# A gated linear-attention layer with a complex feed-forward layer: squares on ScalarE, grouped edge copies, a causal mask made in two places, and sums of squares in column tiles

## The reference

```
mixed = x @ W_qkv.T                      # 3072 channels: q, k, v, 16 heads of 64 each
mixed = silu(causal depthwise conv, 4 taps, of mixed)
q, k = l2norm(q) * 64**-0.5, l2norm(k)   # per head
beta = sigmoid(x @ W_b.T); g = -exp(A_log) * softplus(x @ W_a.T + dt_bias)
S_t = S_{t-1} * exp(g_t) + k_t (v_t * beta_t)^T ;  o_t = q_t S_t
out = o * rsqrt(mean(o*o) + 1e-6) * silu(x @ W_z.T);  y = out @ W_out.T
ffn: W_real, W_imag (512 x 512) unfolded from small factors;
     out_real = xr @ Wr.T - xi @ Wi.T + bias_real, out_imag = xr @ Wi.T + xi @ Wr.T + bias_imag
```

## Time and profile before

| | us |
|---|---|
| median of 3 runs (lowest, highest) | 971.15 (971.06, 973.98) |
| the profiled execution, its own time | 975.45 |
| its span, slowest core (7) | 973.7 |
| PE, DVE, POOL, ACT busy on core 7 | 737.8, 461.4, 274.6, 264.9 |
| mean granted TensorE clock, core 7 | 0.900 |

### The profile page before, as it was taken

One profiled execution on the slowest core, in us unless ns is written; L12 is line 12 of the kernel. 1 busy time (PEld: TensorE's weight loads), 2 busy tenths in 40 slices (PEclk: granted clock), 3 DMA queues, 4 the chain that ended last, 5 costly groups with the idle time before them and its releaser, 6 DMA issues.

```text
span 973.7 us, 15242 instructions; the slowest of 8 cores (947.4 to 973.7 us)
## 1 busy us (share of the span) xinstructions
PE 737.8 (76%) x4912; PEld 337.0 (35%) x4912; DVE 461.4 (47%) x716; ACT 264.9 (27%) x445; POOL 274.6 (28%) x551
## 2 busy tenths in 40 slices
PE   0345768787877977978784888899879999787755
PEld 0111323343433432424331334344333444344311
DVE  0623345574845665525420534654436455455522
ACT  0121232342333423322331232233223334221100
POOL 2023213315133233142312342313244133222210
PEclk9967869999999979999997979899979999977777
DMA  5876555565465773635767525437526345422311
GB/s 122 166 158 140 114 140 168 131 163 163 130 163 131 182 189 110 196 117 136 149 171 190 180 61 152 123 107 191 148 77 163 87 122 150 113 77 78 76 54 54
DMA packets 113285, 129.98 MB, mean 133 GB/s; under 512 B 56228, under 2 KB 76588, under 8 KB 113072
## 3 DMA queue, kind: packets, MB, share of 16 engines
q1 hardware_dynamic: 103056, 107.78, 39.9%
q0 software_dynamic: 10144, 21.15, 11.8%
HBM read 110.02 MB, written 18.27 MB: 132 GB/s over the span
## 4 chain that ended last, share of the span: by engine, by line
PE 54%; DVE 11%; DMA 11%; issue 8%; ACT 6%; POOL 6%; SPq 2%; DVEq 0%; POOLq 0%; ACTq 0%
PE pR L448 23%; PE pR L506 10%; PE pB L862 5%; POOL s_ksq L519 4%; PE pA L896 4%; DMA wscr<-s_w 4%; ACT s_post L512 2%; DVE s_ktil L685 2%; DMA s_lnxT<-s_lnx 2%; DMA dscr<-s_d 2%; SPq L131 2%; ACT L512 1%; DVE s_pre L480 1%; ACT L397 1%; PE pB L760 1%
## 5 line engine op out<-in xcount | busy, mean ns | idle before, releaser
L448 PE MATMUL pR<-s_lnxT,s_w 128*128 128x512 bf16 x1408 | 341.0, 396 | 26.7 <-DMA s_w<-wcat 13.8
L448 PEld LDWEIGHTS pR<-s_lnxT,s_w 128*128 128x128 bf16 x1408 | 136.9, 101 | 195.6 <-issue 58.0
L506 PE MATMUL pR<-s_pre,s_d 128*128 128x512 bf16 x608 | 166.2, 409 | 24.0 <-DVE s_pre L480 14.2
L480 DVE CAST s_pre<-pR 128x512 bf16<-128x512 f32 x152 | 104.3, 687 | 64.8 <-PE pR L448 64.7
L512 ACT ACTIVATE s_post<-pR 128x512 bf16<-128x512 f32 x152 | 86.2, 596 | 133.8 <-PE pR L506 133.4
L483 POOL COPY s_halo<-s_pre 128x3 bf16<-128x3 bf16 x152 | 47.0, 309 | 260.9 <-DVE s_pre L480 254.2
L512 ACT ACT_TABLE_LOAD x32 | 41.1, 1283 | 197.7 <-PE pR L506 197.7
L506 PEld LDWEIGHTS pR<-s_pre,s_d 128*128 128x128 bf16 x608 | 54.7, 102 | 100.5 <-issue 50.8
L519 POOL TENSOR_TENSOR s_ksq<-s_post 128x512 bf16<-128x512 bf16 x64 | 67.4, 1061 | 53.7 <-ACT s_post L512 51.6
L816 DVE TENSOR_TENSOR s_S<-s_S,pA 128x512 f32<-128x512 f32 x32 | 21.9, 685 | 124.5 <-POOL s_S L793 103.4
L492 PE MATMUL pG<-s_ksq,s_bones 128*32 128x128 bf16 x256 | 16.7, 248 | 81.3 <-POOL s_ksq L519 81.3
(11 more groups left out here) (124 smaller groups left out, 814.2 us busy)
## 6 DMA issues: line engine op xcount, KB each, us to landing
s_w<-wscr SPq DMA_DIRECT2D x144, 256.0 KB, 3.4
s_d<-dscr SPq DMA_DIRECT2D x128, 128.0 KB, 3.8
s_xa<-x SPq DMA_DIRECT2D x30, 512.0 KB, 4.6
s_w<-wcat POOLq DMA_DIRECT2D x32, 256.0 KB, 5.3
wscr<-s_w SPq DMA_DIRECT2D x32, 256.0 KB, 3.8
s_x<-x SPq DMA_DIRECT2D x14, 512.0 KB, 4.6
s_rb<-rscr POOLq DMA_DIRECT2D x24, 256.0 KB, 4.7
y<-s_x SPq DMA_DIRECT2D x12, 512.0 KB, 3.0
```

Of the source, the lines that this page charges most:

```text
L448: ins = P.e.matmul(ps, w[:, dc * 128:(dc + 1) * 128], lnxT[u % 2][:, dc, :], start=(dc == 0), stop=(dc == 7))
L480: te = V.mark(V.e.tensor_copy(out=pre[sl][:, 3:515], in_=ps))
L506: ins = P.e.matmul(ps, dr[i % ND][:, tap * 128:(tap + 1) * 128], pre[sl][:, tap:tap + 512], start=(tap == 0), stop=(tap == 3))
```

## The change

- Squares of k move to ScalarE, behind their silu (`AF.Square`). `ksq` gets 4 buffers. `k2_flush(left)` now leaves two pending in `conv`; what is left of a step is flushed after the first `proj` of the next, and `gates_c` moves behind that.
- `pre` becomes one tensor of 7 slots, one for each block of a step. VectorE copies all of a step's halos in at its start (`halo_in`) and out after its last `proj` (`halo_out`).
- The mask: 64 more rows in the decay product (115 rather than 51) carry -57344 wherever the column is smaller than twice half the row number, rounded down; the second matmul goes. What is left of the triangle GpSimd sets to zero after the exponential with an `affine_select` of 128x1024.
- Sums of squares go to four column tiles of 32, at 128 rows. `ssb`, `r32` and the stored `rscr` become 128 rows high.
- The bias is added on GpSimd to the residual (128x1024 float32) before `ffn`, whose two last matmuls go.
- `state_decay` is a function of its own and is called before `qk`.
- `boot` issues x, the first weight and five constants before the branch; the coefficient of `prow` is made after the first tile's norms. 
- In a step `tvk` comes before `ln2_norm`, `decay(n,0)` and `qtil` before `r_load`, and one more `proj` between the two decays.

```
-NW, ND, NP, NK = 5, 6, 8, 3
+NW, ND, NP, NK = 5, 6, 7, 4
+            bones[par * 64:(par + 1) * 64, cc, 16 * (cc % 2) + par] = 1.0
+    blk = np.tile(np.repeat(np.eye(64, dtype=np.float32), 2, axis=1), (1, 4))
+    mrow = np.tile(np.where(np.arange(128)[None, :] < 2 * np.arange(64)[:, None],
+                            np.float32(MASKNEG), np.float32(0.0)), (1, 16))
...
+    def boot():
+        for m in range(4):
+            begin(nc.sync, f"qxa{m}", x2[m - 2] if m in (2, 3) else xa[m],
+                  d_x[m * 128:(m + 1) * 128, :])
+        begin(nc.gpsimd, "qwc0", wr[0], d_w[8])
+        begin(nc.gpsimd, "qc0", wab.rearrange("p a b -> p (a b)"), d_wab)
+        begin(nc.sync, "qc1", i128f, d_i128)
+        begin(nc.sync, "qc2", cw.rearrange("p a b -> p (a b)"), d_cw)
+        begin(nc.sync, "qc3", prow[:, 0:6], d_prow)
+        begin(nc.gpsimd, "qc4", bones32.rearrange("p a b -> p (a b)"), d_bones32)
...
+        def halo_in(u, E):
+            k = len([cc for cc in E if not own_halo(u, cc)])
+            V.need(*[conv_tok[x] for x in pre_user if x is not None])
+            if k:
+                p0 = spos(u, E[0])
+                V.need(halo_saved[0])
+                halo_tok[u] = V.mark(V.e.tensor_copy(out=pre[:, 0:k, 0:3],
+                                                     in_=halo[:, p0:p0 + k, 0:3]))
+
+        def halo_out(u, E):
+            p0, k = spos(u, E[0]), len(E)
+            V.need(evac_tok[(u, E[-1])], halo_tok[u])
+            halo_saved[0] = V.mark(V.e.tensor_copy(out=halo[:, p0:p0 + k, 0:3],
+                                                   in_=pre[:, 0:k, 512:515]))
...
-            th = G.mark(G.e.tensor_copy(out=pre[sl][:, 0:3], in_=halo[:, cc, 0:3]))
...
-            G.need(te, th)
-            pre_saved[(u, cc)] = G.mark(G.e.tensor_copy(out=halo[:, cc, 0:3],
-                                                        in_=pre[sl][:, 512:515]))
...
-            k2_flush()
+            k2_flush(2)
             if 8 <= cc < 16:
                 kb = ksq_i[0] % NK
                 ksq_i[0] += 1
-                G.need(silu_tok[(u, cc)], ksq_user[kb])
-                ksq_tok[(u, cc)] = G.mark(G.e.tensor_tensor(
-                    out=ksq[kb], in0=post[u % 2][:, cc, :], in1=post[u % 2][:, cc, :],
-                    op=ALU.mult))
+                S.need(silu_tok[(u, cc)], ksq_user[kb])
+                ksq_tok[(u, cc)] = S.mark(S.e.activation(
+                    out=ksq[kb], in_=post[u % 2][:, cc, :], func=AF.Square))
...
-                P.e.matmul(pq, b3[t % 2][:, c * 128:(c + 1) * 128], ih[:, par, :, :],
-                           start=True, stop=False)
-                ins = P.e.matmul(pq, mnegT, itile4, start=False, stop=True)
+                ins = P.e.matmul(pq, b3[t % 2][:, c * 128:(c + 1) * 128], ih[:, par, :, :],
+                                 start=True, stop=True)
...
+            G.need(fr[0][0])
+            d3 = dd.rearrange("p (a b) -> p a b", a=8)
+            exp_tok[(n, h2)] = G.mark(G.e.affine_select(
+                out=d3, in_=d3, pattern=[[0, 8], [1, 128]], compare_op=ALU.is_ge, fill=zero_reg,
+                base=0, channel_multiplier=-1))
...
+                for w_, o_ in ((bones, o2.rearrange("p (a b) -> p a b", a=8)), (bonesq, qsq)):
+                    for cc in (0, 2, 4, 6, 1, 3, 5, 7):
+                        q0 = 32 * (cc // 2)
+                        ins = P.e.matmul(pA[q0:q0 + 32, 512:640], w_[:, cc, :], o_[:, cc, :],
+                                         start=(w_ is bones and cc % 2 == 0),
+                                         stop=(w_ is bonesq and cc % 2 == 1),
+                                         tile_position=(0, q0))
...
+        def add_bias(n):
+            G.need(norm2_tok[n], late["bias"])
+            xb_tok[n] = G.mark(G.e.tensor_tensor(out=x2[n % 3], in0=x2[n % 3], in1=biasb,
+                                                 op=ALU.add))
...
-            P.e.matmul(pA[:, 0:512], onesr[0:1, :], biasb[0:1, :], start=False, stop=True)
-            ffn_tok[n] = P.mark(P.e.matmul(pA[:, 512:1024], onesr[32:33, :], biasb[32:33, :],
-                                           start=False, stop=True))
...
                 fe(1)
+                k2_flush(0)
+                if streaming and s == 2:
+                    gates_c(u)
+                if att:
+                    tvk(g)
                 if on2:
                     ln2_norm(n2)
-                if att:
-                    tvk(g)
                 fe(1)
+                if own:
+                    decay(n, 0)
+                    qtil(n)
+                fe(2)
+                ln1_norm(m)
                 if on1:
                     r_load(n1)
                 if own:
-                    decay(n, 0)
-                    qtil(n)
-                fe(1)
-                ln1_norm(m)
-                if own:
                     decay(n, 1)
+                if on2:
+                    add_bias(n2)
                 if streaming and s == 2:
                     gates_d(u)
                 fe(8)
+                if att:
+                    state_decay(g)
```

More of the change, by code:

```diff
@@ L98, with __init__ @@
 class Lane:
-    def __init__(self, eng, sem):
+    def __init__(self, eng, name, sem):
         self.e = eng
+        self.name = name
         self.h = sem
@@ L186, in build_program @@
     lnxT = [sb(f"s_lnxT{i}", [128, 8, TT]) for i in range(2)]
-    pre = [sb(f"s_pre{i}", [128, 516]) for i in range(NP)]
+    pre = sb("s_pre", [128, NP, 516])
     halo = sb("s_halo", [128, 24, 4])
@@ L208, in build_program @@
     S_b = sb("s_Sb", [128, 512])
-    ind51 = sb("s_ind51", [51, 2048])
-    b3 = [sb(f"s_b3{i}", [51, TT]) for i in range(2)]
+    ind51 = sb("s_ind51", [115, 2048])
+    b3 = [sb(f"s_b3{i}", [115, TT]) for i in range(2)]
     ga = sb("s_ga", [128, 128], F32)
@@ L259, in slots, with begin @@
     def slots(name, n):
-        return [Slot(sem(f"{name}{i}")) for i in range(n)]
+        return [Slot(f"{name}{i}", sem(f"{name}{i}"), f"{name}{i}" in begun) for i in range(n)]
+    begun = set()
+    def begin(eng, name, out, in_):
+        eng.dma_start(out=out, in_=in_).then_inc(sem(name), 16)
+        begun.add(name)
+    def boot():
[8 more added lines that the diff above has]
+        begin(nc.gpsimd, "qc4", bones32.rearrange("p a b -> p (a b)"), d_bones32)
     def emit(NPRE, NOWN):
         NT = NPRE + NOWN
-        P = Lane(nc.tensor, sem("mP"))
-        V = Lane(nc.vector, sem("mV"))
-        S = Lane(nc.scalar, sem("mS"))
-        G = Lane(nc.gpsimd, sem("mG"))
-        Y = Lane(nc.sync, sem("mY"))
+        P = Lane(nc.tensor, "mP", sem("mP"))
+        V = Lane(nc.vector, "mV", sem("mV"))
+        S = Lane(nc.scalar, "mS", sem("mS"))
+        G = Lane(nc.gpsimd, "mG", sem("mG"))
+        Y = Lane(nc.sync, "mY", sem("mY"))
         q_w, q_wc, q_ws = slots("qw", NW), slots("qwc", NW), slots("qws", NW)
@@ L451, in proj_mm, with proj @@
             return i, k, ps, t
-        def proj(u, cc):
-            if u == NPRE > 0 and cc < 8:
+        def proj(u, cc, j):
+            if own_halo(u, cc):
                 i = w_pos[(u, cc)]
@@ L980, in emit @@
         ln1_stats(4)
+        S.need(t_prow)
+        t = S.mark(S.e.activation(out=prow[:, 7:8], in_=prow[:, 2:3], func=AF.Exp))
+        V.need(t)
+        t_coef = V.mark(V.e.tensor_scalar(out=prow[:, 6:7], in0=prow[:, 7:8], scalar1=-1.0,
+                                          scalar2=None, op0=ALU.mult))
         E_own = [[8, 9, 10, 11, 12, 13, 14], [15, 16, 17, 18, 19, 20, 21],
@@ L1015, in fe @@
                         if E:
-                            proj(u, E.pop(0))
+                            j = len(E0) - len(E)
+                            proj(u, E.pop(0), j)
                             uf(RATE)
+                            if not E:
+                                halo_out(u, E0)
                 def fc(k=1):
                     for _ in range(k):
-                        if C and C[0] not in E:
-                            conv(u, C.pop(0))
+                        if C:
+                            j = len(E0) - len(C)
+                            conv(u, C.pop(0), j)
                 def fz(k=1):
```

182 lines of the change are left out of this document (80 added, 102 removed).

## The result

The changed kernel takes 1070.5 us (median of 4 runs, 1068.3 to 1077.8); the kernel before took 971.1 beside it. The ratio is 1.103 (95% interval 1.097 to 1.109): 10% slower, where 877 us, 9.7% faster, was predicted.

A forecast was written before the change was run, and what follows sets the result against it. PE's own work was taken to bound tiles 6 and 7, its waits for other engines the rest; 13 + 17 + 22 + 14 + 35 - 7 = 94 us off 975.45 gave 881.5, median 877, range 850 to 918.

The forecast's parts named there:

- last stretch: Core 7 after the last streamed work: 7 us lost, as rb is loaded behind select and qsq; bounds 2 gained, 15 lost.
- a select over 3 us: Sign that the forecast is wrong: GpSimd's select in the attention steps takes over 3 us, where 1.2 to 1.9 was expected.
- first tile: Core 7, 40.6 to 138.5 us: 17 us gained as PE stops waiting for GpSimd; bounds 5 and 25.
- an even core is the slowest: Sign that the forecast is wrong: in the whole kernel, an even core has the longest span.
- Even against odd: Whole kernel: the even core (949.4) wins over 80 us, more than the 69 needed, so the odd core stays slowest.
- tiles 6 and 7: Core 7's eight streamed attention steps: 35 us gained from shorter waits and less PE work; bounds 22 and 45.
- start: Core 7 before PE's first matmul: 13 us gained by early issues, PE beginning at about 27.6; bounds 7 and 17.
- tiles 1 to 4: Core 7: 22 us gained, PE's wait for squares falling from 4.0 to 1.3 us per group; bounds 10 and 32.
- tile 5: Core 7: 14 us gained from squares, halo copies and a state decay; bounds 5 and 20.
- Refilled gaps: Rival, first tile and tile 5: store chains and loads set their length, both give 0; 915 us, chance 0.17.
- ScalarE as the late one: Rival, tiles 1 to 7: squares delay silus and PSUM buffers, only half the squares' waits won; about 897 us, chance 0.09.
- the select as the slower case: Rival, attention steps: GpSimd's select far dearer than 1.5 us; at 9 us, 44 slower, 1015 us; chance 0.04.

The follow-up runs named there:

- Contiguous: The changed kernel with rows of r stored so that the eight rows one load of rb reads lie side by side: 908.3 us, ratio 0.938 to before.
- the product early: Contiguous kernel with VectorE's product q x exp(D) moved to right after tvk, before ln2_norm and decay(n,0): 882.5 us, ratio 0.909 to before.

## Why the prediction failed, point by point

**The step that failed** is in the part on the last stretch: "the larger r (128 rows) beside the same DMA latency". The eightfold rows were taken as more bytes to store; nothing in the prediction looked at how the load reads them. The runs showed a load that lands in 12.0 us instead of 4.8, and this cost 162 us (1070.5 against 908.3). None of the rivals had it: a select over 3 us and a first tile near 98 us did not come. The sign "an even core is the slowest" did, and even cores have the more attention steps, where the loss is.

**Even against odd.** The prediction gave even cores over 80 and left the odd one slowest. Contiguous, the longest even span is 906.3, 44 less than before. The step that failed here is that VectorE's durations were taken as fixed; the product alone has 36 us more on core 4 (49.7 against 13.6 busy). With it moved, the longest even span is 879.0, 72 less than before, and an odd core is the slowest again.

**The sum, on core 7 of the contiguous kernel.** From the window view, tiles 6 and 7 and the last stretch, cut at the last streamed matmul:

```profile
471.90:742.90 271.00, 251.45 (x1847) 116.73 (x1847) 160.74 (x219) 103.78 (x174) 88.88 (x95) 0.97 0.55 147
742.90:888.30 145.40, 79.71 (x577) 37.38 (x575) 68.19 (x73) 20.66 (x40) 46.95 (x44) 0.69 0.25 68
```

| term | predicted | measured |
|---|---|---|
| start | 13 | 7 (40.6 to 33.5) |
| first tile | 17 | 9 (97.9 to 88.6) |
| tiles 1 to 4 | 22 | 36 (265.1 to 229.1) |
| tile 5 | 14 | 11 (131.5 to 120.7) |
| tiles 6 and 7 | 35 | 34.5 (305.5 to 271.0) |
| last stretch | -7 | -12 (133.1 to 145.4) |
| sum | 94 | 85 |

The size is near, the owners are partly wrong. Tiles 1 to 4 gained more than the upper bound of 32. They were sized by ScalarE's own time against a flush thought to keep 1.3 us of wait per group; the late flush took nearly all of it. With the flush as before they take 253.0 us on core 7, so 24 of the 36 are the flush's. The working has two slips besides: 6.7 less 2.9, 0.4 and 1.8 leaves 1.6 of wait and not 1.3, and in the last stretch 2.8 + 1.5 + 1.9 is 6.2 and not 6.5.

The start was mis-sized twice. The first transpose does go at 16, as forecast. The second goes at 18.7, but its issue takes SyncE 6.01 us, where before it took 1.23, and VectorE's next norm waits for the transposes:

```profile
16.24 1.77 SPq L140 DMA_TRANSPOSE s_lnxT<-s_lnx  x1
...
18.74 6.01 SPq L140 DMA_TRANSPOSE s_lnxT<-s_lnx  x1
...
26.98 0.81 DVE L430 TENSOR_SCALAR s_lnx<-s_x,s_bnA 128x1024 bf16<-128x1024 f32 x1 [6.72 <-DMA s_lnxT<-s_lnx]
```

So the 9.6 us from the second transpose to PE's first matmul, taken over from before, became 14.8. Of the 7 gained the early issues have 3.4 (36.9 to 33.5), and the run without them is no slower.

In the last stretch 12 us were lost on core 7, not 7, though the select was cheaper than taken. The prediction priced a later load of `rb`; with the load early, the four odd cores take 143 us there, and contiguous they take 142 to 146. With the mask by matmuls they take 135 to 137, where the kernel before takes 133 to 137, and its four products all take 0.68 us; with the product early, 138 to 139. So the loss in this stretch is the select's, the greater part of it through the product that it meets; the bias add has no part in it (147 to 148 without it).

**The select** takes 1.11 us in the median, 0.4 under the 1.5 taken. By the line rate that the Trainium skill, "GPSIMD Engine Reference" (section 4.1), gives one-input operations, the prediction's estimate was near 1: the runs agree. The price of branching there (section 3.1) does not show in it.

**The rivals.** Refilled gaps came in part: half of the first tile's gain is missing, with the DMA engines busy 0.81 of it instead of 0.61, but tile 5 gained 11 of the 14. ScalarE as the late one is not borne out: the convs on core 7 wait 6.8 us in all for a silu, 0.9 at most. The select as the slower case fell.

What stays open: which of the moved steps bring the rest of the 62 us (the flush accounts for 26), why ScalarE's squares cost 11 in one kernel and nothing clear of noise in another, and why the distance of 8 KB costs 162 us here and 43 in the kernel before.

## What to carry to other kernels

When a change alters a tensor's height, write out the addresses of every load that reads it: small rows 8 KB apart cost more here than all that the change saved, and storing them side by side took the cost away. Work moved to GpSimd is not free for VectorE: place VectorE's instructions with two SBUF inputs where GpSimd does not read SBUF, before asking which engine should have the work. Where an engine waits for a result, first move the reader later; moving the producer to another engine may then be needless. And when stages of two kernels are compared, cut them at the same event.

## What the runs showed of the hardware

- Reading eight rows of 512 bytes, each spread over many partitions, 256 KB per load, landed in 4.8, 7.1 and 10.7 us at distances of 1, 4 and 8 KB in one kernel; in the other it took 12.0 at 8 KB, 5.6 at 9 KB and 4.7 with the rows side by side. The slow loads held back others: with the distance alone changed from 1 to 8 KB, the transposes of `lnx` went from 5.3 to 11.7 us, a 4 KB store from 3.3 to 11.2.
- A VectorE product of 1024 bf16 columns took 0.68 us alone and up to 4.85 beside GpSimd instructions that read SBUF; each of the 13 lengthened ended 0.54 to 0.56 us after one of these.
- GpSimd's affine select of 128x1024 bf16 took 1.11 us, its add of 128x1024 float32 2.13, ScalarE's square of 128x512 0.63.
- The mean granted clock of core 4 was 0.848 in the changed kernel, with PE busy 67% of the span, and 0.891 contiguous, with 76%.
